# A graph network's edge stage on one Trainium2 core, laid out anew: message matrix stationary on the two column halves, counts spread over 194 groups, node sums written by DMA

## The reference, cut to what matters

```python
def _L0_gnn_ref(p, idx_i, idx_j, basis, ...):
    p1 = jnp.tanh(p @ pp_W1 + pp_b1) @ pp_W2 + pp_b2
    inter = jnp.concatenate([p1[idx_i], p1[idx_j]], axis=-1)
    inter = (inter @ pi_W1 + pi_b1) @ pi_W2 + pi_b2
    inter = (inter @ pi_W3).reshape(n_edges, 64, 8)
    i1 = jnp.einsum('ecb,eb->ec', inter, basis)
    i1 = jnp.tanh(i1 @ ii_W1 + ii_b1) @ ii_W2 + ii_b2
    return jax.ops.segment_sum(i1, idx_j, num_segments=p1.shape[0])
...
x = x + _L0_gnn_ref(h, src, dst, edge_attr_8, ...)
x = x + _L1_gnn_ref(h, ...)     # three layers: agg = segment_sum(h[src], dst), then @ W.T
x = x + _L2_gnn_ref(...)        # three layers of segment_sum(norm * x[src], dst)
x = x + _L3_gnn_ref(...)        # one segment_sum(x[src], dst) and a small network
```

## Time and profile before

| | |
|---|---|
| median of the runs | 6523.84 us |
| the profiled execution: time | 6531.14 us |
| its span | 6529.4 us |
| instructions recorded | 137592 |
| TensorE busy | 6144.8 us (94%) |
| TensorE weight loads busy | 4186.5 us (64%) |
| POOL busy | 3865.4 us (59%) |
| DVE busy | 3031.9 us (46%) |
| ACT busy | 1898.0 us (29%) |
| message products (L982), PE records | 12544, mean 270 ns |
| messages' products z (L815) | 1576, mean 680 ns |
| gathers of the edge stage (L695) | 1576, mean 1115 ns |
| casts of counts (L735) | 2080, mean 670 ns |

### The profile page before, as it was taken

How to read it: one execution, slowest core, us unless ns; L and a number is a source line. 1 busy time by engine, 2 the same in 40 slices (tenths; PEclk the granted TensorE clock), 3 DMA queues, 4 the chain that set the end, 5 groups by cost and what they waited for, 6 DMA issues and landing times.

```text
span 6529.4 us, 137592 instructions
## 1 busy us (share of the span) xinstructions
PE 6144.8 (94%) x43472; PEld 4186.5 (64%) x43472; DVE 3031.9 (46%) x6076; ACT 1898.0 (29%) x3108; POOL 3865.4 (59%) x3728
## 2 busy tenths in 40 slices
PE   0779999999999999999799999999999999999999
PEld 0458888888888888888645555555555555555555
DVE  5478888888888888755422211222311111112101
ACT  1446666666666666511000000000000000000000
POOL 1146666666666666666376566566476567565565
PEclk9679999999999999999699999999999999999999
DMA  4233433333333333322388888888888888888886
GB/s 145 72 93 116 117 120 116 118 119 116 117 117 120 115 118 120 106 75 74 83 291 317 291 319 313 298 317 314 297 317 316 301 317 319 311 319 300 305 292 240
DMA packets 480554, 1350.46 MB, mean 207 GB/s; under 512 B 236738, under 2 KB 264930, under 8 KB 418277
## 3 DMA queue, kind: packets, MB, share of 16 engines
q1 hardware_dynamic: 271924, 1146.43, 48.1%
q0 software_dynamic: 118656, 176.66, 10.6%
q10 hardware_dynamic: 89620, 22.76, 1.7%
HBM read 1170.31 MB, written 175.21 MB: 206 GB/s over the span
## 4 chain that ended last, share of the span: by engine, by line
PE 50%; issue 0%; POOL 0%; ACT 0%; DVE 0%; ACTq 0%; DVEq 0%
PE ps_a L1627 46%; PE ps_t L1670 1%; PE ps_t L1668 1%; PE ps_w L1589 1%; PE ps_t L1647 0%; PE ps_t L1672 0%; PE ps_a L1579 0%; POOL hb L1277 0%; POOL table L1279 0%; POOL table L1275 0%; ACT agg L1319 0%; POOL hb L1273 0%; PE ps_w L1600 0%; DVE h L112 0%; ACT agg L1315 0%
## 5 line engine op out<-in xcount | busy, mean ns | idle before, releaser
L1627 PE MATMUL ps_a<-ring,table 128*128 128x448 fp8e4 (+1 forms) x15778 | 3063.7, 353 | 50.7 <-POOL table L1279 33.5
L1267 POOL DMA_INDIRECT rows<-table_rows,gather_plan x2072 | 1997.3, 964 | 1203.5 <-issue 579.7
L695 POOL DMA_INDIRECT gathered<-u_source,plan x1576 | 1757.0, 1115 | 1178.1 <-issue 617.2
L1627 PEld LDWEIGHTS ps_a<-ring,table 128*128 128x128 f16 x15778 | 1514.1, 98 | 1391.9 <-issue 49.1
L982 PEld LDWEIGHTS ps_m<-M_sb,z 128*128 128x128 f32 x12544 | 1604.7, 192 | 111.1 <-issue 4.2
L735 ACT CAST unit<-ps_c 128x490 fp8e4<-128x490 f32 (+1 forms) x2080 | 1393.8, 670 | 736.3 <-PE ps_c L917 730.2
L982 PE MATMUL ps_m<-M_sb,z 128*128 128x64 f32 x12544 | 1573.3, 270 | 0.0
L815 DVE TENSOR_TENSOR z<-ps_b,u 128x512 f32<-128x512 f32 x1576 | 1067.7, 680 | 269.8 <-ACT u L724 203.4
L1446 DVE TENSOR_TENSOR far_agg<-far_agg,ps_w 128x64 f32 x518 | 114.8, 222 | 2127.7 <-PE ps_w L1589 2113.1
L1315 ACT COPY agg<-ps_a 128x448 f32<-128x448 f32 (+1 forms) x161 | 85.3, 530 | 2764.4 <-PE ps_a L1627 2764.4
L917 PE MATMUL ps_c<-cell_hot,lane_hot 128*128 128x490 f16 x2080 | 743.3, 370 | 0.0
(11 more groups left out here) (234 smaller groups left out, 2983.4 us busy)
## 6 DMA issues: line engine op xcount, KB each, us to landing
ring<-counts SPq DMA_DIRECT2D x462, 1848.0 KB
counts<-unit SPq DMA_DIRECT2D x160, 792.0 KB, 3.9
dst_all<-dst_local SPq DMA_DIRECT2D x198, 256.0 KB
ring<-counts SPq DMA_DIRECT2D x21, 1584.0 KB
rows<-table_rows,gather_plan POOLq DMA_INDIRECT x2072
gathered<-u_source,plan POOLq DMA_INDIRECT x1576
table_rows<-table ACTq DMA_DIRECT2D x49, 448.0 KB
window<-u_target SPq DMA_DIRECT2D x396, 32.0 KB
```

The costliest lines, as they stand in the source:

```text
L695: pool.indirect_dma_start(gathered[q][:, i, :, :].rearrange("p s d -> p (s d)"), None, Us, bass.IndirectOffsetOnAxis(ap=T["plan"][:, at:at ...
L1267: pool.indirect_dma_start(rows[:, s, t, :], None, G["tables"][n % 2], bass.IndirectOffsetOnAxis(ap=T["gather_plan"][:, at:at + 1], axis=0) ...
L1627: last = mm(ps_a[:, b, 0:width].rearrange("p (u c) -> p u c", c=UC), table[n % 2][:, k, :], cells, start=(k == 0), stop=(k == TILES - 1))
```

## The change

Only `edges` and the tables for it in `prepare` change.

- **M product.** The roles are swapped: a part of M (128 x 64) is stationary and 512 edges of z move, so the result has features on partitions. Half 0 of the group goes to the array's columns 0 to 63 and partitions 0 to 63 of `ps_m`, half 1 to columns and partitions 64 to 127. That is 8 matmuls of 512 columns for a group instead of 32 of 64 (16 float32 records instead of 64), in two pieces (k = 0, 1 and k = 2, 3) with other work between. The bias matmul falls away: ACT adds the bias in the tanh (`msgT`). Four transposes (`turn`) bring the result back to edges on partitions, and one more ACT copy (`take_msg`) writes `msg`.
- **Node sums.** A fifth tile stands ahead of each half's four: the tile before it, so that nodes which straddle two halves are whole in the later one (`to_node` has 10 tiles instead of 8, 10 matmuls instead of 8). ACT copies `ps_w` to `stage` (`take_sums`) and SyncE writes it over `aggT` by DMA (`write`), one write after the other; DVE's additions and its register loads fall away.
- **Counts.** The 2080 blocks are spread evenly over 194 groups, 10 or 11 in each, in 8 shares. A unit is stored when its last block is cast.
- **Order and control.** Every engine's order within a group is new, `join` is split (half 0 two groups ahead), waits have new semaphores, the gathers wait half by half, and all loops are unrolled.

Cut to its core:

```diff
+COUNT_GROUPS = EGROUPS - 2
+COUNTED = UD * UB
+blocks_before = lambda g: COUNTED * min(max(g, 0), COUNT_GROUPS) // COUNT_GROUPS
...
-        ps_m = ps("ps_m", [P, ET, D])
+        ps_m = ps("ps_m", [P, EH])
...
+        def blocks(g, i):
+            first, n = blocks_before(g), blocks_before(g + 1) - blocks_before(g)
+            return range(first + n * i // 8, first + n * (i + 1) // 8)
...
+                def write(g):
+                    bases = [base_of(sp, g, h) for h in range(2)]
+                    sp.wait_ge(S["staged"], g + 1)
                     for h in range(2):
+                        if g or h:
+                            sp.wait_ge(S["written"], 16 * (2 * g + h))
+                        sp.dma_start(aggT[:, bass.ds(bases[h], W)], stage[g % 2][:, h, :]).then_inc(S["written"], 16)
...
+                for s in range(-3, EGROUPS + 2):
+                    load_rows(s + 2)
+                    load_targets(s + 3)
+                    load_window(s + 3)
+                    if inside(s):
+                        keep(s)
+                    write(s - 1)
...
+                    nc.scalar.activation(msgT[:, :], ps_m[:, :], ACT.Tanh, bias=T["bias"][:, :]).then_inc(S["tanh"], 1)
...
+                    nc.scalar.copy(rows_of(g % 2), turned).then_inc(S["msg_out"], 1)
...
+                    nc.scalar.copy(stage[g % 2][:, :, :], ps_w[0:D + 1, :, :]).then_inc(S["staged"], 1)
...
+                for s in range(-2, EGROUPS + 2):
+                    take_msg(s - 1)
+                    empty(s, 0, 1, 2, 3)
+                    take_u(s + 1, 1)
+                    empty(s, 4, 5)
+                    apply_tanh(s)
+                    empty(s, 6)
+                    take_sums(s - 1)
+                    empty(s, 7)
+                    take_u(s + 2, 0)
...
-                        nc.vector.tensor_tensor(there, there, ps_w[0:D + 1, h, :], ALU.add).then_inc(S["added"], 1)
...
+                for s in range(-2, EGROUPS):
+                    multiply(s + 1, 0, 1)
+                    place_cells(s + 1, 0)
+                    place_to(s)
+                    multiply(s + 1, 2, 3)
+                    place_from(s + 2)
+                    place_cells(s + 1, 1, 2)
+                    multiply(s + 1, 4)
+                    place_cells(s + 1, 3, 4, 5)
+                    place_lanes(s + 1)
+                    multiply(s + 1, 5)
+                    place_cells(s + 1, 6, 7)
+                    multiply(s + 1, 6, 7)
...
-                        mm(ps_m[:, :, :].rearrange("p t d -> p (t d)"), T["bias_ones"][:, :], T["bias_rows"][:, :, :].rearrange("p t d -> p (t d)"), start=True, stop=False)
...
-                                last = mm(ps_m[:, i, :], z[2 * q + h][:, k, i % HT * P:(i % HT + 1) * P], T["M"][:, k, :], start=False, stop=(i == ET - 1 and k == 3))
...
+                def apply_m(g, *parts):
+                    for k in parts:
+                        if k == 0 and g:
+                            pe.wait_ge(S["msg_out"], g)
+                        pe.wait_ge(S["z_done"], 8 * g + 4 + k + 1)
+                        for h in range(2):
+                            last = mm(ps_m[D * h:D * h + D, :], T["M"][:, k, :], z[2 * (g % 2) + h][:, k, :], start=(k == 0), stop=(k == 3))
...
+                def turn(g):
+                    pe.wait_ge(S["tanh"], g + 1)
+                    for j in range(HT):
+                        last = nc.tensor.transpose(ps_m[:, j * P:(j + 1) * P], msgT[:, j * P:(j + 1) * P], T["ident"][:, :])
...
+                for s in range(-2, EGROUPS + 2):
+                    turn(s - 1)
+                    count(s, 0)
+                    copy_basis(s + 1, 0)
+                    count(s, 1)
+                    join(s + 1, 1)
+                    copy_basis(s + 1, 1, 2)
+                    count(s, 2)
+                    apply_m(s, 0, 1)
+                    copy_basis(s + 1, 3)
+                    count(s, 3)
+                    copy_basis(s + 1, 4)
+                    count(s, 4, 5)
+                    apply_m(s, 2, 3)
+                    count(s, 6)
+                    copy_basis(s + 1, 5)
+                    add_up(s - 1)
+                    count(s, 7)
+                    copy_basis(s + 1, 6)
+                    join(s + 2, 0)
+                    copy_basis(s + 1, 7)
```

More of the change, by code:

```diff
@@ L1 @@
+import itertools
 import numpy as np
@@ new lines, in take_sums, with empty @@
+                def take_sums(g):
+                    if not inside(g):
+                        return
+                    act.wait_ge(S["summed"], g + 1)
+                    if g >= 2:
+                        act.wait_ge(S["written"], 32 * (g - 1))
+                    act.sem_inc(S["passed"], 1)
+                    nc.scalar.copy(stage[g % 2][:, :, :], ps_w[0:D + 1, :, :]).then_inc(S["staged"], 1)
+                def empty(g, *shares):
+                    if not inside(g):
+                        return
+                    for b in itertools.chain(*(blocks(g, i) for i in shares)):
+                        v, i = b // UB, b % UB
+                        if i == 0 and v >= 2:
+                            act.wait_ge(S[f"kept{v % 2}"], 16 * (v // 2))
@@ L990, in regular, with copy_basis @@
-                with pe.Fori(0, UD // 2) as t:
-                    step(t, True)
-                with pe.Fori(UD // 2, STEPS) as t:
-                    step(t, False)
-                for h in range(2):
-                    sum_half(1, STEPS, EGROUPS, h)
+                    last.then_inc(S["joined"], 1)
+                def copy_basis(g, *parts):
+                    if not inside(g):
+                        return
+                    for n in parts:
+                        if n == 0:
+                            pe.wait_ge(S[f"basis_in{g % 2}"], 16 * (g // 2) + 16)
+                        if 8 * g + n >= 2:
+                            pe.wait_ge(S["z_done"], 8 * g + n - 1)
+                        pe.sem_inc(S["passed"], 1)
+                        mm(ps_b[n % 2][:, :], T["pick"][:, n % 4, :], basis[g % 2][:, 512 * (n // 4):512 * (n // 4) + 512], start=True, stop=True).then_inc(S["copied"], 1)
```

429 lines of the change are left out of this document (186 added, 243 removed).

## The result

The changed kernel takes 6177.0 us, the median of 4 runs (6170.6 to 6188.6), against 6525.4 us for the kernel before (4 runs, 6516.8 to 6531.8). The ratio is 0.947, its 95% interval 0.945 to 0.949: 348 us faster. The forecast was 6340 us, 184 us faster; the sign holds and the gain was put at about half its size.

What follows compares the result with a forecast made beforehand. TensorE was taken to bound the edge stage: 11.9 us of work plus 1.0 of waits and 0.1 unseen gave 13.0 us a group, 196 groups plus 33 us making 2581, so 6340 us in all; range 6262 to 6438 us.

Steps and rivals of the forecast that it cites:

- rival 2: Edge stage: the count burst costs little or sums run at 1.2 us; 12.0 us a group, 6144 us; chance 0.15 below 6262.
- the wide range: Whole kernel time, 6160 to 6740 us, said to hold 0.8 of the chance.
- M and switching: TensorE, per group: two M pieces of 2.15 us with halves overlapped, 4.3 us, plus two switches in and out, 0.5 us.
- waits, and what can't be seen: TensorE, per group: 1.0 us waiting for ACT's casts before counts, plus 0.1 us for what the trace hides.
- five slots: M piece on TensorE: eight records, starts in program order, take five slots rather than four, 2.15 us a piece.
- a count burst that costs little: TensorE's counts between M pieces: their waits cost little, one of two ways to 12.0 us a group.
- The wait that comes: Counts on TensorE wait for ACT to free two banks: 1.2 us with 11 blocks, some 0.6 with 10, 1.0 on average.
- the fill and drain: Start and end of the edge stage, outside its 196 group periods: 33 us.
- Hidden engines: Per group beside TensorE: DVE 10.8 us, ACT 9.3, POOL 11.6, SyncE's queue near 8, all within the period.
- Rival 1: M's halves don't run side by side: M 6.8 us, period 15.5 us, time 6830 us; chance 0.22.
- The harder form: M's halves don't overlap and weight loads are exposed too: 9.1 us for M, 17.8 a group, 7280 us; chance 0.02.
- Rivals 3 and 4: Edge stage: engine chain adds 0.5 to 0.9 us, 6438 to 6511 us, chance 0.10; or within 0.07 us of break-even, 0.05.

## Why the prediction was right, and where its size was off

The mechanism is the forecast's: M's two halves run side by side, TensorE stays the bound, and the counts between the pieces wait for ScalarE's casts. The size is not. A period of 12.30 us lies outside the forecast's 12.6 to 13.5 and falls under rival 2, "it goes better", which had a chance of 0.15; the 6177 us are near the lower end of the wide range, 6160. By its terms, in us a group (measured by distances between starts, 1000 to 1500 us):

| term | forecast | measured |
|---|---|---|
| joins and copies | 3.1 | 3.1 |
| counts | 2.1 | 2.2 (0.21 each) |
| sums | 1.5 | 1.18 |
| transposes | 0.45 | 0.44 |
| M and switching | 4.3 + 0.5 | 3.4 + 0.5 |
| waits, and what can't be seen | 1.1 | 1.5 (the rest of 12.30) |

- **M.** Forecast were five slots of 0.43 a piece and 0.25 for the switch; measured are four slots, and for the switch 0.09 in front and 0.15 to 0.16 behind, which is what the earlier trace rows gave. So the slots are the term that was mis-sized most, 0.86 us a group or 170 us, and the switch was sized right. The slots failed on the sentence that a half's records hold up the other half's; the order of starts had been read from traces with one stream only. The record itself was sized right from the earlier trace rows: 0.43 measured.
- **Sums.** 1.18 us for twenty records. The value 1.5 was taken between two bounds, and the lower one (1.2), from eight records in a row, was the right reading: 0.32 us a group or 63 us. This half of rival 2 came true; its other half, a count burst that costs little, did not, and it did not name the slots of M.
- **The wait that comes.** Right in place and cause, a little small: 1.3 us a group between the pieces where 1.0 was forecast, and 0.1 ahead of the first one. Behind the second piece the changed kernel hardly waits. That place, where the next counts need a cast that stands behind the tanh, becomes a wait only when the burst is gone: 1.21 us in the group shown of the run with the counts spread.
- **Sum of errors.** -0.86 (M) - 0.32 (sums) + 0.1 (counts) + 0.4 (waits) = -0.7, from 13.0 to 12.3; the errors partly cancel. 196 x 0.7 = 137 us. Most of the rest to 163 us is the fill and drain, put at 33 us: the stage of 2416 us holds 196 x 12.30 = 2411.
- **Hidden engines.** DVE is busy 88% of the 500 us (forecast 83% of a longer period), 10.8 us a group as forecast. GpSimd is busy 69%, and 87% with its issue time (forecast near 90%); it waits for TensorE's joins 66 us in 500, so it is hidden, as costed. The writes on SyncE hide too: ScalarE's wait for them doesn't stand among its waits. The dense stage is the same.
- **What the gain is made of.** By the same distances, M with its bias went from 6.9 us a group to 3.9, and the transposes took 0.44 back; the sums and the branch gave two tenths each, and the waits cost over 1 us. The M product is the only term as large as the gain, 13.94 to 12.30 on average. Its halves side by side are shown by the run on one half of the columns; the shares of the other edits in the 348 us are read from distances, and no run in the quick condition takes them away one by one.
- **Rival 1** fell, and its price was about right: one half of the columns gives 16.03 us in a group at full clock, forecast 15.5. The harder form fell with it. Rivals 3 and 4, a longer period and no change, fell with the time. The Trainium skill, TensorE: Matmul & The Clock Gate, The mechanism, has a load overlap a running matmul only if the row groups differ; here they are the same, and the trace differs from that: in the run on one half of the columns a load starts with nearly every record and lies beside it, and eight records with their loads take 3.58 us, 0.45 each, so the loads cost next to nothing. The Trainium skill, TensorEngine Tiling (Array Packing), Key Properties, has different tiles run in parallel; by that the trace agrees, 1.87 us against 3.58, and it agrees that changing the mode has a price, 0.09 us in and 0.15 to 0.16 out.

## What to carry to other kernels

A float32 product with a stationary of 64 columns uses half the array: two such streams on the two halves of columns and partitions cost as much as one, in both orders that were tried here. Once TensorE's work is shortened, the next bound is not an engine's busy share but the order in another engine's row: count, for each two-bank exchange, what stands between one cast and the next, on past the stretch that you edited. And time a change beside the kernel before, on the same chip and at the same time, since the same edit was worth 5.3% in one condition and 3% in the other.

## What the runs showed of the hardware that was not expected

- Matmuls of two column halves start in pairs 0.43 us apart even when four records of one half stand ahead of the other's in the program.
- A switch to a stationary of 64 columns and back costs 0.25 us beside 128-column products: 0.09 in front of the first record, 0.15 to 0.16 behind the last.
- A chip can be in a condition in which the kernel before takes 9075 us and not 6527: the unedited kernel's run and the two quick ones stand under the same chip number, eight minutes apart. In it TensorE, VectorE and ScalarE stand at once for some 6 us in most groups of the changed kernel. In the group shown the recorded clock is 1.00 until 2018, while they already stand, and 0.50 from 2020 to 2024. What stops them, why it comes behind the first M piece, and why the kernel before gains 4 to 5% there by unrolling, stays open.
